# Two wide cross-attention layers run as one sequence, and three layer-norm roots moved to VectorE

## What is computed

```python
res = x
h = _layer_norm(x, ln1_scale, ln1_offset)
x = res + _cross_attention(h, xf_1, wq1, bq1, wk1, bk1, wv1, bv1, wo1, bo1, bias_k1, bias_v1)
res = x
h = _layer_norm(x, ln2_scale, ln2_offset)
x = res + _cross_attention(h, xf_2, wq2, bq2, wk2, bk2, wv2, bv2, wo2, bo2, bias_k2, bias_v2)
h = _layer_norm(x, ln_mlp_scale, ln_mlp_offset)
h = jax.nn.gelu(h @ w_fc1 + b_fc1, approximate=False) @ w_fc2 + b_fc2
return x + h
```

## Time and profile before

| | us |
|---|---|
| median of 3 runs | 2492.37 (2485.69 to 2496.15) |
| the profiled execution, its own time | 2487.22 |
| span of the profiled execution | 2485.2 |
| PE busy in it | 2187.6 |
| DVE busy in it | 1781.9 |
| ACT busy in it | 1446.2 |
| POOL busy in it | 710.6 |

### The profile page before, as it was taken

The page is one execution under the profiler, slowest core; times in us unless marked ns, Lnnn a source line. Parts: engine busy times, 40 slices in busy tenths (PEclk is TensorE's granted clock), DMA queues, the critical chain, the costliest instruction groups (busy, mean ns, idle before and its releaser), DMA issues. The chain is left out here.

```text
span 2485.2 us, 52655 instructions
## 1 busy us (share of the span) xinstructions
PE 2187.6 (88%) x17289; PEld 1768.5 (71%) x17289; DVE 1781.9 (72%) x4649; ACT 1446.2 (58%) x4000; POOL 710.6 (29%) x1041
## 2 busy tenths in 40 slices
PE   4999999994999999996978888689989697788888
PEld 3998989994998989996955555456666496555554
DVE  7666666667666666667658888698888664677776
ACT  2554545553554555555637676577777674577765
POOL 3011111111011111103034554466666502433300
PEclk9999999996999999998969999799999998799999
DMA  4001111000000110002000000100000000000001
GB/s 123 22 22 23 22 23 56 22 22 22 1 23 22 22 22 22 1 1 67 0 10 10 10 9 4 35 8 1 9 20 16 7 1 7 8 10 8 7 3 35
DMA packets 72948, 47.22 MB, mean 19 GB/s; under 512 B 29232, under 2 KB 71600, under 8 KB 72752
## 3 DMA queue, kind: packets, MB, share of 16 engines
q1 hardware_dynamic: 72752, 44.62, 6.8%
HBM read 41.45 MB, written 2.10 MB: 18 GB/s over the span
## 5 line engine op out<-in xcount | busy, mean ns | idle before, releaser
L1791 DVE TENSOR_REDUCE maxima<-bank 128x2 f32<-128x512 f32 x512 | 342.3, 683 | 103.2 <-PE bank L952 101.0
L1468 ACT ACTIVATE probs_t<-bank 128x512 f32<-128x512 f32 x512 | 282.4, 601 | 73.7 <-PE bank L943 70.9
L1344 ACT ACTIVATE wide_probs_t<-bank 128x256 f32<-128x256 f32 x256 | 98.5, 385 | 310.6 <-PE bank L832 308.4
L2128 POOL TENSOR_TENSOR wide_columns<-wide_pair_columns,zero 128x8 f32<-128x8 f32 x16 | 3.3, 204 | 862.2 <-DVE x L1688 821.0
L1349 ACT ACTIVATE wide_probs<-bank,wide_neg_max 128x129 f32<-128x129 f32 x512 | 184.1, 365 | 84.3 <-DVE wide_neg_max L1658 80.0
L1356 ACT ACTIVATE wide_heads_high<-bank,wide_columns 128x128 fp32r<-128x128 f32 x512 | 160.3, 365 | 96.0 <-PE bank L844 94.7
L1663 DVE RECIPROCAL wide_inverse<-wide_sums 128x2 f32<-128x2 f32 x256 | 42.4, 166 | 224.4 <-ACT wide_probs L1349 224.4
L1677 DVE SCALAR_TENSOR_TENSOR wide_heads_low<-bank,wide_columns,wide_heads_high 128x128 fp32r<-128x128 f32 x512 | 155.1, 344 | 41.2 <-ACT wide_heads_high L1356 35.9
L943 PE MATMUL bank<-q_packed,k_packed 32*128 32x256 f32 x1024 | 170.4, 331 | 8.1 <-ACT probs_t L1468 7.4
L1504 ACT ACTIVATE probs<-scores_masked,neg_max 128x128 f32<-128x128 f32 x512 | 163.3, 394 | 24.0 <-DVE neg_max L1978 22.4
L1665 DVE TENSOR_SCALAR wide_probs<-wide_probs,wide_inverse 128x128 f32<-128x128 f32 x512 | 170.4, 375 | 9.0
(11 more groups left out here) (294 smaller groups left out, 6832.4 us busy)
## 6 DMA issues: line engine op xcount, KB each, us to landing
cn<-in_ctx SPq DMA_DIRECT2D x48, 128.0 KB, 2.0
wide_pair_weights<-in_L_xattn_wq SPq DMA_DIRECT2D x16, 256.0 KB, 2.8
wide_pair_weights<-in_L_xattn_wk SPq DMA_DIRECT2D x16, 256.0 KB, 3.2
wide_pair_weights<-in_L_xattn_wv SPq DMA_DIRECT2D x16, 256.0 KB, 3.6
wide_pair_weights<-in_L_xattn_wo SPq DMA_DIRECT2D x16, 256.0 KB, 3.5
q_packed<-max_rows SPq DMA_DIRECT2D x256, 4.0 KB
wide_ctx_rows<-in_ctx SPq DMA_DIRECT2D x4, 512.0 KB, 4.3
x<-in_x SPq DMA_DIRECT2D x4, 512.0 KB, 5.4
```

The costliest lines, as they stand in the source:

```text
L1468: act.activation(probs_t[j % 8][:, :], shifted_bank[j % 2][:, :], ACT.Exp, bias=0.0).then_inc(s.exp_ready, 1)
L1791: dve.tensor_reduce(maxima[pack // 2][:, b, pack % 2, :], head_scores[packed_scores(1 - u, j)][:, :].rearrange("p (a k) -> p a k", a=UNITS ...
```

## The change

1. The two wide layers become one sequence of 64 windows. `over_groups` lists 0 to 63; the loops cover windows 1 to 24 (three times 8) and 41 to 56 (two times 8), and 25 to 40 and 57 to 63 are written out. Window 31 now projects for window 32, as every other does.
2. The second layer's norm is done inside the windows. `second_group(g, back)` gives the group n for which a step is due in window g. DVE: in windows 29 to 32, mean and variance behind batch 1, the root behind batch 2, the normalized rows behind batch 3 (`norm_second`). PE and ACT: in windows 30 to 33, one half (two batches) behind batch 1 and one behind batch 2 (`turn_half`, `split_half`), through the banks of `wide_heads`. POOL: the rest of the rounding and the second layer's output bias, in `second_low`, between its splits of pairs 8 and 9. PE waits for each group's rest in windows 31 to 34.
3. The first layer's norm: three groups are normed before window -1, the fourth between window -1 and window 0. The first layer's output bias is added in four parts inside window 0. SP loads the first pair's weights behind the first two groups of context and x; ACT rounds them, POOL only takes the rests, and POOL's split of pair 1 waits until the fourth group is done.
4. Last packed attention: for the first three batches (`FIRST_ROWS`) DVE takes the root and writes `norm_packed` (`first_rows`); POOL goes on with the fourth.

```diff
-def over_groups(engine, window):
+def over_groups(engine, window, between):
+    span = 2 * GROUPS
+    last = 2 * PAIRS * GROUPS
...
     window(-1, -1, 0, False, False, True)
+    between(0)
     window(0, 0, 0, True, False, True)
-    span = 2 * GROUPS
-    with engine.Fori(0, PAIRS // 2 - 1) as i:
-        for k in range(1, span + 1):
-            window(span * i + k, k, 2 * i, True, True, True)
...
+    between(1)
+    looped(1, last // 2 - span + 1)
+    fixed(last // 2 - span + 1, last // 2 + span + 1)
+    looped(last // 2 + span + 1, last - span + 1)
+    fixed(last - span + 1, last)
+    window(last, span, last // GROUPS - 2, False, True, False)
...
+def second_group(g, back):
+    n = g - (SECOND - GROUPS + 1 + back) if isinstance(g, int) else -1
+    return n if 0 <= n < GROUPS else None
...
+        def turn_half(g, half, b):
+            r = GROUPS + g
+            pe.wait_ge(rows_normed, GROUP * (r + 1))
+            for c in range(DC):
+                for m in range(2):
+                    last = pe.transpose(wide_heads[b % 2][:, c * D + m * P:c * D + (m + 1) * P], wide_rows[:, 2 * half + m, c * P:(c + 1) * P], ident[:, :])
+            last.then_inc(normed_turned, 1)
...
+                ready, turning = second_group(g, 2), second_group(g, 1)
...
+                    if ready is not None and b == 0:
+                        pe.wait_ge(normed_low_ready, DC * (GROUPS + ready + 1))
...
+                        if turning is not None and b >= 2:
+                            pe.wait_ge(normed_ready, DC * (GROUPS + turning) + b - 1)
...
+                    if turning is not None and b in (1, 2):
+                        turn_half(turning, b - 1, b)
...
+        def split_half(g, half, b):
+            act.wait_ge(normed_turned, DC * r + half + 1)
+            act.wait_ge(normed_low_ready, DC * (r - 1) + half + 1)
...
+            for c in range(DC):
+                ins = act.activation(normed[:, c, part], wide_heads[b % 2][:, c * D:(c + 1) * D], ACT.Identity, bias=norm_offset[:, 1, c:c + 1],
+                                     scale=norm_scale[:, 1, c:c + 1])
...
+        def norm_second(g, b):
+            if b == 1:
+                dve.wait_ge(rows_normed, GROUP * r)
+                dve.wait_ge(x_added, 2 * (SECOND - GROUPS + g) + 2 + ADD_CREDIT)
+                moments(dve, chain, group_rows(g), stats, idle)
+            elif b == 2:
+                chain.steps = 2 * GROUP
+                inverse_root(dve, chain, stats.rstd[:, :], stats.mean_var[:, :, 1], stats.shifted[:, :], stats.work[:, :])
+            else:
+                normalize_group(r, g)
...
+                    if core and not carry:
+                        first_bias(b)
+                    if ended is not None and b:
+                        norm_second(ended, b)
...
+        def second_low(g):
+            pool.wait_ge(rows_normed, GROUP * (r + 1))
+            pool.tensor_tensor(rows, rows, row_bias[:, 1:2, :].broadcast_to([P, GROUP, D]), ALU.add).then_inc(preparation_steps, 1)
+            for half in range(2):
...
+                pool.wait_ge(normed_high_ready, DC * r + half + 1)
+                pool.tensor_tensor(low, normed[:, :, part], high.bitcast(F32), ALU.subtract).then_inc(normed_low_ready, 1)
...
+            if layer:
+                split_pair(PAIRS, 0)
+                for g in range(GROUPS):
+                    second_low(g)
+                split_pair(PAIRS + 1, 1, GROUPS)
...
+            def first_rows(b, u):
+                inverse_root(dve, chain, stats.rstd[:, :], stats.mean_var[:, :, 1], stats.shifted[:, :], stats.work[:, :])
+                after(dve, s.turned_back, b - 1)
+                for k in range(4):
+                    ins = dve.tensor_scalar(norm_packed[u][:, k // 2, k % 2 * P:(k % 2 + 1) * P], turned_packed[u][:, k, :],
+                                            stats.mean_var[:, k, 0:1], stats.rstd[:, k:k + 1], ALU.subtract, ALU.mult)
...
+                    if isinstance(i, int) and i + 4 < FIRST_ROWS:
+                        dve.wait_ge(s.aggregated, 4 * (i + 5))
+                        first_rows(i + 4, u)
...
         load_context(1)
         load_x(1)
+        load_pair(0, 0, 0)
```

More of the change, by code:

```diff
@@ L280, in row_statistics @@
     chain.join()
+def row_statistics(dve, chain, rows, stats, idle):
+    n = len(rows)
+    moments(dve, chain, rows, stats, idle)
     inverse_root(dve, chain, stats.rstd[:, 0:n], stats.mean_var[:, 0:n, 1], stats.shifted[:, 0:n],
@@ L1280, in feed_forward3 @@
                         back3(r + 1, h)
-        for layer in range(2):
-            norm_and_split(layer)
-            pairs(layer)
+        norm_and_split()
+        pairs()
         feed_forward(0)
@@ L2385, in _ @@
         for layer in range(2):
-            with sp.Fori(0, PAIRS) as q:
+            with sp.Fori(0 if layer else 1, PAIRS) as q:
                 load_pair(layer, PAIRS * layer + q, q)
```

250 lines of the change are left out of this document (151 added, 99 removed).

## The result

The changed kernel takes 2465.85 us (median of 4 runs, 2457.16 to 2466.64), the kernel before 2493.55 us (4 runs, 2485.69 to 2496.15) in the same comparison: a ratio of 0.9886 with a 95% interval of 0.9855 to 0.9918. It is faster by 1.1%. The forecast was 2459 in a range of 2443 to 2476. The profiled execution took 2457.16 us with a span of 2455.2 (before: 2487.22 and 2485.2); it is the shortest of the four.

A forecast was written before the change was run, and what follows sets the result against it. PE bounds the wide windows, except a hole where DVE norms the second layer alone. Savings of 26.2 (middle), 2 (start) and 5 (packed attention) make 33 us: execution 2487.2 to 2454, median 5.2 above, so 2459, range 2443 to 2476.

The forecast's parts named there:

- DVE as the bound of windows 29 to 32: Windows 29 to 32: with the second layer's norm DVE needs 19.08 us in each, PE 16.7.
- Window 33 on PE: Window 33 has the transposes but no norm, so PE bounds it at 16.7 us.
- POOL's share: Windows 29 to 33: `second_low` on POOL slows DVE, 3.3 us by proportion to the split, bounds nothing and 6.7.
- Rival 1: POOL and DVE exclude each other fully: 3.3 becomes 20.5, time 2484, half of it 2471; 10% for 2470 to 2486.
- the middle: Start of window 29 to that of 34: 96.3 us against 121.8, 25.5 saved, 26.2 with two more terms.
- Loop returns: The loop has one return less, so window 41 falls from 17.34 to 14.98 us, 2.36 back.
- The start: Up to window 1: first maxima at 52.0, window 0 lasting 20.3, window 1 at 72.3; 2 us saved.
- The bound below, -4: Lower bound of the start's gain: earlier weight loads could make the third group 5.4 us late, 1.7 becoming -3.7.
- The packed attention: Last packed attention: first scores 9.0 us earlier, third root takes 4.1 back; 5 saved, bounds 0 and 13.5.
- The clock: PE's granted clock should be 1.00 from 550 to 700; clocks of 0.50 there would show the prediction wrong.
- rival 2: PE's clock falls to 0.50 in DVE-bound windows: four cost 57 us, kernel 24 slower, 2516; 4%.
- Rival 3: Transposes, ACT halves and their waits hit PE in turn: eight places of 1.5 us, 12 us, 2471; 8%.

The follow-up runs named there:

- run 1: Changed kernel with nine of the eleven root instructions of the second norm left out; windows 31 and 32 lasted 18.51 and 18.52 us.
- run 2: Changed kernel with each transpose of the second norm's halves issued twice; windows 30 to 32 lasted 19.96, 19.84 and 19.83 us, window 33 18.02.
- run 8: Packed-attention roots on DVE: none or two in the changed kernel, three in the kernel before; with two 2455.39 us, 0.9853 of the kernel before.
- run 6: Changed kernel with POOL's second split no longer waiting for all four groups' normed rows; window 0 lasted 19.18 us, window 1 began at 78.12.
- run 7: Changed kernel with first pair's weights loaded behind the third group, or fourth group's norm ahead of the values; first maxima at 57.11 and 49.65 us.
- run 3: Changed kernel with POOL's second-norm bias add cut to one column; windows 30, 31 and 32 lasted 19.98, 19.97 and 20.75 us.
- run 4: Changed kernel with second norm's statistics and root, and window 0's bias, moved into waits for exponentials; single execution 2452.20 us.
- run 5: Changed kernel with waits filled, fourth group's norm earlier and POOL's three instructions per group cut into eight; 2448.49 us, 0.9823 of the kernel before.
- run 9: Changed kernel with waits for exponentials filled and the fourth group's norm ahead of the values; 2454.85 us, 0.9840 of the kernel before.

## Why the prediction held, point by point

**DVE as the bound of windows 29 to 32: right.** 19.08 us were forecast for DVE alone, window 29 took 19.40, and run 1 takes off exactly what DVE is spared. The 0.3 are one wait of 0.33 us for `wide_heads_high` of ACT, which windows 30 to 32 don't have.

**Window 33 on PE: right.** 17.15 for 16.7, and it grows with the transposes, by 0.87 for eight (run 2).

**POOL's share: the right term, too small, and with a wrong rule.** It was 3.3 us, by proportion to POOL's busy time. Windows 30 to 32 lasted 1.7 to 1.8 us more than the 19.08 of DVE alone, 5.3 together, and window 33 has 0.45. The step that failed is "by proportion to the split": the price is two hits in a window, 0.86 on the probabilities and 0.99 on a root step, each the rest of one POOL instruction. Rival 1 had the mechanism right and the price wrong: it took all of POOL's time as lost, 20.5, but DVE loses only what is left of an instruction when it comes to need the lock. The trace of the kernel before already had this price: beside POOL's first split, steps of the fourth group's root took 0.89 to 1.11 us instead of 0.16, one for each instruction of POOL, as here:

```profile
34.15 1.11 DVE L266 SCALAR_TENSOR_TENSOR stat_work<-rstd 128x4 f32<-128x4 f32 x1
```

With the 0.3 of window 29 that is 6.05 where 3.3 stood, and the middle gave 22.75 instead of 25.5. POOL's split of pair 9, priced at 1.64 in windows 33 and 34, cost 0.94 in window 34 and part of the 0.45 in window 33.

**Loop returns: right in place, uncertain in size.** Window 41 gave back its 2.36 in every kernel with the one sequence (14.98). But windows 9, 17 and 49, behind returns that stayed, lasted 17.1 to 20.2, 17.0 to 20.3 and 15.5 to 17.6 from one profiled execution to the next.

**The start: wrong by its whole size.** 2 us were forecast, with window 1 at 70 to 74. Window 1 began at 74.94, 1.0 later than before, and lasted 1.2 less; window 2 begins 0.2 earlier in the profiled execution, as in two others with the same start (89.58, 89.61), and 1.9 to 2.3 *later* than before in three more (91.57, 91.69, 91.92); the same start of the kernel before gave 89.66 and, in run 8, 90.61. The bound below, -4, held them. Three parts of the sum were off. The third group was turned at 33.86, not at 30.2, for two reasons. Its context comes later: SP issues the ten loads of the first pair ahead of it, so its own issue is at 12.80 instead of 6.92, PE waits for it, and DVE is done with it 1.3 us later, counted from the rows that it normalized before. That is the lateness that the prediction named for its bound of -4, at a quarter of the size. And POOL's four subtractions for the first pair now stand beside DVE's. In the changed kernel, PE, POOL and DVE at that place:

```profile
19.72 1.97 PE L781 MATMUL bank<-ident,wide_ctx_rows 128*128 128x128 f32 x8 [3.73 <-DMA wide_ctx_rows<-in_ctx]
...
20.31 5.54 POOL L2289 TENSOR_TENSOR wide_weights_low<-wide_pair_weights,wide_weights_high 128x512 fp32r<-128x512 f32 x4 [2.02 <-ACT wide_weights_high L1387]
...
22.36 0.69 DVE L1651 TENSOR_TENSOR wide_ctx_low<-bank,wide_ctx_high 128x512 fp32r<-128x512 f32 x1 [0.16 <-ACT wide_ctx_high L1350]
22.96 3.44 DVE L1715 TENSOR_TENSOR wide_normed_low<-wide_normed,wide_normed_high 128x512 fp32r<-128x512 f32 x2
```

Two subtractions of 0.6 us each took 3.44, 2.2 more than before; this lock at the start was not in the sum at all. Window -1, from its first product to the fourth group's first statistic, was 1.75 shorter than assumed, 9.9 us, and window 0 took 21.41 to 22.7, not 20.3: POOL's split there costs 2.2 or more (run 6), where 1.6 had been taken, and part of PE's slow products moved from the one to the other (last section). The gain that was found lay in the order of the norm (run 7); what the place of the loads is worth stays open.

**The packed attention: right.** 5.7 for 4.9; in the other two pairs of executions 5.2 (before, with the roots and without) and 6.1 (changed, without and with). Its least certain part, that the third root takes 4.1 back by standing ahead of `k_low`, measured 4.08.

**The clock: right in its price, not in what would be seen.** The prediction wanted 1.00 from 550 to 700 and named clocks of 0.50 as a sign of being wrong. Such a stretch is there: near the end of window 30 PE waited 1.84 us for DVE, and behind that the granted clock was 0.50.

```profile
570.43 0.44 PE L881 MATMUL bank<-ident,wide_probs 128*128 128x128 f32 x2 [1.84 <-DVE wide_probs L1766]
```

```profile
571.00:573.00 2.00, 2.00 (x6) 1.54 (x5) 2.00 (x7) 0.29 (x1) 0.00 (x0) 0.50 0.00 0
```

So what rival 2 starts from did happen, for some 3 us at a time instead of a whole window, and nearly free of charge. In six executions nothing is changed in windows 30 to 32. PE waits 1.8 us at the end of each of them, and the clock fell behind some of these waits and not behind others: it was 0.91 to 1.00 by windows. The windows lasted 20.80 to 20.91 in all six, the one with 1.00 throughout (20.91, 20.80, 20.81) included: DVE is the bound, and where the clock had fallen PE lacked its next wait of 0.9 us instead. It cost something once, in window 32 of run 3, whose windows are shorter. In runs 1, 2, 4, 5 and 9 the clock stayed at 1.00 there; what decides it, no run shows. Rival 3 had no place: with PE's turns doubled windows 30 to 32 did not grow.

**The sum.** Profiled execution against profiled execution 33 was forecast and 30.0 came: 24.2 for 26.2 in the middle (22.75, less 0.94, and 2.36), 0.2 for 2 at the start, 5.7 for 5. What else differs between the two executions, 1.1 and 1.0 won, 1.4 and 0.9 lost, cancels; that is luck, as its parts are as large as the errors of the terms. The median moved less, 27.7: the profiled execution was the shortest of four, and the median stands 8.7 above it where 5.2 had been assumed. From the last window to the first placed row, code that no run changed, the profiled executions took 964.8 to 973.6 us, and this one 964.8. What varies there was not found.

## What to carry to other kernels

Work hidden beside a bound engine is priced by what the *other* engine has free, waits for its own round trips included: when DVE became the bound, its waits of 0.88 us for each exponential were the first thing worth filling, and moving the same instructions into them was worth 8 us (3.1 at the start, 4.9 in the middle), beside the 30 of the whole change. Where DVE and GpSimd work side by side, don't multiply busy time by a factor: list which DVE instruction begins while a GpSimd one runs, and charge the rest of that instruction; put GpSimd's work where DVE reads PSUM or waits, and cut it into short instructions. And when steps move from a slow engine to a fast one, stop at the step that stands ahead of what the next engine waits for: two roots moved brought the scores 9.8 us nearer where three brought them 5.7.

## What the runs showed that was not expected

Eight more transposes in a window on PE made it 1 us shorter, because they shifted a GpSimd instruction past a 4-column DVE instruction; without that hit it is the same window. And PE's clock, which fell to 0.50 in some executions of the windows bound by DVE, cost these windows nothing, until one of them was made shorter.

A DVE instruction of 0.16 us can stand for 1.15, and a GpSimd instruction too waits its turn: copies of the weights that take 1.03 us took 2.12 where DVE's bias add of 1.21 began at the same moment (window 0 of the changed kernel):

```profile
58.66 2.12 POOL L2251 TENSOR_TENSOR wide_weights_high<-wide_pair_weights,zero 128x512 fp32r<-128x512 f32 x1
...
62.08 1.03 POOL L2251 TENSOR_TENSOR wide_weights_high<-wide_pair_weights,zero 128x512 fp32r<-128x512 f32 x1
...
58.67 1.21 DVE L1737 TENSOR_TENSOR x<-x,row_bias 128x1024 f32<-128x1024 f32 x1
```

When PE has waited at the start, its first products pass at half pace: one 128x512 product every 0.43 us instead of every 0.23. In the kernel before this lasted from 48.00 to 53.1, and it went on for five microseconds of unbroken work:

```profile
52.43 0.63 PE L739 MATMUL bank<-wide_normed_low,wide_weights_high 128*128 128x512 f32 x1
52.86 0.46 PE L740 MATMUL bank<-wide_normed_high,wide_weights_low 128*128 128x512 f32 x1
53.16 0.47 PE L738 MATMUL bank<-wide_ctx_high,wide_weights_high 128*128 128x512 f32 x1
53.47 0.40 PE L739 MATMUL bank<-wide_ctx_low,wide_weights_high 128*128 128x512 f32 x1
```

In the changed kernel it lasted 1.3 us at the head of window -1, behind a wait of 6.97, and 2.6 us at the head of window 0, behind 6.22. By these spacings half of the difference between 5.1 and 1.3, 1.9 us, is what window -1 should have become shorter by, and it was 1.75; half of 2.6, 1.3 us, is what window 0 can have become longer by, beyond the sum. The granted clock doesn't show it alike: for the stretch from 48 to 60 us of the kernel before its row has 1.00, for 43 to 53 of the changed kernel 0.60.

```profile
48.00:60.00 12.00, 12.00 (x56) 9.98 (x57) 7.43 (x6) 1.57 (x4) 6.37 (x7) 1.00 0.17 27
```

```profile
43.00:53.00 10.00, 3.15 (x13) 2.75 (x14) 7.24 (x28) 2.59 (x4) 0.00 (x0) 0.60 0.00 0
```

So the start is read from the spacing of the products, not from the clock's row. What sets the length of the slow part, no run here tells.
